# Attention's first norm, fronts, rotations and maxima placed in the first feed-forward's last two batches, and no filling periods

## The reference

```python
x = x + 0.5 * ffn(layernorm(x), ...)     # 2 shared and 8 routed experts, top 2 of 8, capacity 1280
x = x + attn(layernorm(x), ...)          # 16 heads of 64, rotary + Fourier terms, softmax
x = x + 0.5 * ffn(layernorm(x), ...)     # same weights as the first

# in attn, with scale = 64 ** -0.5:
q = q * cos + rotate_half(q) * sin + fenc
k = k * cos + rotate_half(k) * sin + fenc
out = softmax(q @ k.T * scale) @ v        # per head
return out_of_all_heads @ w_out.T + b_out

# in ffn, for every expert:
h = silu(x @ gate.T) * (x @ up.T)         # times the token's share for a routed expert
y += h @ down.T
```

## Time and profile before

| | |
|---|---|
| median of 3 runs | 1315.5 us (1313.26 to 1315.73) |
| the profiled execution | 1315.65 us, its span 1313.9 us |
| busy share | PE 97%, DVE 64%, ACT 47%, POOL 67% |
| granted TensorE clock, mean | 0.987 of full |

### The profile page before, as it was taken

One profiled execution on the slowest core, in us unless ns is written; L12 is line 12 of the kernel. 1 busy time (PEld: TensorE's weight loads), 2 busy tenths in 40 slices (PEclk: granted clock), 3 DMA queues, 4 the chain that ended last, 5 costly groups with the idle time before them and its releaser, 6 DMA issues.

```text
span 1313.9 us, 21618 instructions
## 1 busy us (share of the span) xinstructions
PE 1268.6 (97%) x7858; PEld 790.6 (60%) x7858; DVE 840.1 (64%) x1352; ACT 614.2 (47%) x917; POOL 883.0 (67%) x652
## 2 busy tenths in 40 slices
PE   5999998699999999999999999999999999999998
PEld 3666665456565656666565656565565655666665
DVE  6656646876666666666666666677786664565632
ACT  3443532255545455545545554545545444443422
POOL 0443444678797888798888888788888862443343
PEclk9999999699999999999999999999999999999999
DMA  5344040223233232323232323323232321442240
GB/s 164 129 177 125 6 130 16 48 42 70 55 66 58 54 70 50 74 50 74 49 74 50 70 54 65 59 54 70 50 74 50 73 34 18 146 137 81 66 153 17
DMA packets 118681, 95.40 MB, mean 73 GB/s; under 512 B 75760, under 2 KB 85008, under 8 KB 118320
## 3 DMA queue, kind: packets, MB, share of 16 engines
q1 hardware_dynamic: 118576, 94.01, 29.8%
HBM read 57.53 MB, written 2.88 MB: 46 GB/s over the span
## 4 chain that ended last, share of the span: by engine, by line
PE 91%; DVE 5%; issue 2%; ACT 1%; DMA 1%; POOL 0%; SPq 0%; DVEq 0%; ACTq 0%
PE banks L1028 17%; PE banks L450 16%; PE banks L1011 13%; PE banks L463 10%; PE banks L1043 7%; PE banks L987 7%; PE banks L952 6%; PE banks L1016 4%; PE banks L1052 4%; PE banks L971 3%; PE banks L994 1%; DVE neg_max L1201 1%; PE banks L412 1%; PE banks L405 1%; PE banks L476 1%
## 5 line engine op out<-in xcount | busy, mean ns | idle before, releaser
L1201 DVE TENSOR_REDUCE neg_max<-banks 128x2 f32<-128x1024 f32 x256 | 313.2, 1224 | 103.1 <-PE banks L987 96.8
L1125 ACT ACTIVATE work<-banks 128x1024 f32<-128x1024 f32 x256 | 250.2, 1025 | 166.6 <-PE banks L1016 166.6
L1303 POOL TENSOR_TENSOR turn<-turn,side_turned 128x512 f32<-128x512 f32 x128 | 160.6, 1275 | 132.4 <-DMA side_turned<-side 132.3
L1028 PE MATMUL banks<-work 128*64 128x512 f32 x1024 | 233.9, 599 | 0.0
L1297 POOL TENSOR_TENSOR turn<-turn,fenc 128x512 f32<-128x512 f32 x128 | 161.9, 1287 | 14.9 <-DVE side L1194 10.9
L1308 POOL TENSOR_TENSOR qk_l<-turn,qk_h 128x512 fp32r<-128x512 f32 x128 | 162.0, 1287 | 0.9 <-ACT qk_h L1130 0.9
L1313 POOL TENSOR_TENSOR work<-work 128x1024 f32<-128x1024 f32 x64 | 152.8, 2387 | 11.2 <-PE banks L1028 11.2
L1028 PEld LDWEIGHTS banks<-work 128*64 128x64 f32 x1024 | 67.8, 136 | 132.9 <-issue 110.1
L987 PE MATMUL banks<-qk_h 64*128 64x512 f32 x512 | 118.0, 455 | 13.2 <-DVE neg_max L1201 10.2
L796 POOL TENSOR_TENSOR turn<-turn,work 128x512 f32<-128x512 f32 x56 | 72.2, 1294 | 87.1 <-DVE turn L717 87.1
L796 POOL TENSOR_TENSOR o_raw<-o_raw,work 128x512 f32<-128x512 f32 x52 | 66.8, 1288 | 89.2 <-DVE o_raw L717 89.2
(11 more groups left out here) (169 smaller groups left out, 2364.6 us busy)
## 6 DMA issues: line engine op xcount, KB each, us to landing
work<-share SPq DMA_DIRECT2D x32, 1024.0 KB, 9.3
side_turned<-side SPq DMA_DIRECT2D x256, 128.0 KB, 3.1
rec_all<-rec_d SPq DMA_DIRECT2D x128, 128.0 KB, 3.3
x_tok<-in_x SPq DMA_DIRECT2D x8, 256.0 KB, 6.1
out<-x_tok SPq DMA_DIRECT2D x8, 256.0 KB, 9.2
work<-in_w_gate_up SPq DMA_DIRECT2D x1, 1280.0 KB, 7.8
work<-in_w_qk SPq DMA_DIRECT2D x1, 1024.0 KB, 9.5
den_d<-den_rows SPq DMA_DIRECT2D x64, 4.0 KB
```

Source lines behind the costliest of these rows:

```text
L1028: ins = nc.tensor.matmul(O[OWN[h], :], v_all[:, kt, n * DH:(n + 1) * DH], pt[:, g % 2, kt, h * T:(h + 1) * T], start=(kt == 0), stop=(kt = ...
L1125: nc.scalar.activation(pt[:, g % 2, kt, :], S[kt].rearrange("p h q -> p (h q)"), ACT.Exp, scale=QSCALE).then_inc(s["probs"], 1)
L1201: nc.vector.tensor_reduce(neg_max[:, g % 2, qt::DH], M2, AX.X, ALU.max, negate=True).then_inc(s["maxes"], 1)
L1303: nc.gpsimd.tensor_tensor(turn[:, g % 2, part], turn[:, g % 2, part], side_turned[:, part], ALU.add).then_inc(done, 1)
```

## The change

The tables move the early work, new ones are added, the three filling periods leave `PERIODS`, and GpSimd gets a hook as well. The set of `qk_h`/`qk_l` that a head pair uses is moved by one (`sets`), and the first feed-forward keeps its fronts the other way round, so that its last chunk leaves `x2_hi` and `x2_lo` to attention; `hid` buffers move from `turn[:, 1]` to `work`. The norm of batches 1 to 5 (20 tiles) is made in the hooks, that of batches 6 and 7 (8 tiles) in periods 4 to 12 (`END_AT`).

```diff
-JOIN_NORM_AT = {46: (0,), 47: (1, 2), 48: (3, 4, 5), 49: (6, 7), 50: (8, 9), 51: (10, 11), 53: (12, 13), 54: (14, 15)}
+JOIN_NORM_AT = {53: (0,), 54: (1, 2), 55: (3, 4, 5), 56: (6, 7), 57: (8, 9), 58: (10, 11), 59: (12, 13), 60: (14, 15)}
...
-        LATER = (B - 1) * TT
+        LATER = 5 * TT
...
-            FILL_FROM = -2 * PAIRS
-            EARLY_NORM_AT = {0: range(0, 4), 1: range(4, 7), 2: range(7, 10), 3: range(10, 13), 4: range(13, 16)}
-            EARLY_FRONT, EARLY_K, EARLY_Q = 5, 7, 8
-            PERIODS = range(-3, N)
-            STATS_AT, SMALL_AT = (-2, -1), (0, 1, 2, 3)
+            PERIODS = range(0, N)
+            QK_FROM, V_FROM = -48, -14
+            EARLY_NORM_AT = {-14: range(0, 4), -13: range(4, 7), -12: range(7, 10), -11: range(10, 13), -10: range(13, 16)}
+            EARLY_FRONT_AT = -9
+            EARLY_PART_AT = {-8: (0, K), -7: (0, Q), -5: (1, K), -4: (1, Q), 9: (2, K), 10: (2, Q)}
+            EARLY_MAXIMA_AT, EARLY_TURN_AT, EARLY_VALUES_AT = (4, 5, 6, 7), 8, (11, 12, 13)
+            EARLY_HIGH_AT = {-1: (0, K), 1: (0, Q), 9: (1, K), 10: (1, Q)}
+            STATS_AT = {-6: range(0, 5), -3: range(5, 10), -2: range(10, 15), -1: range(15, 20)}
+            SMALL_AT = {0: (1, 2), 1: (3, 4), 2: (5, 6), 11: range(7, 11), 12: range(11, LN_STAGES)}
+            END_AT = {4: (0,), 5: (1, 2), 6: (3, 4), 7: (5, 6), 8: (7, 8), 9: (9, 10), 10: (11, 12), 12: (13, 14, 15)}
...
             def early_act(act, k):
-                if FILL_FROM <= k < FILL_FROM + 2 * PAIRS and k % 2 == 0:
-                    qk_high(act, (k - FILL_FROM) // 2)
+                if k >= QK_FROM and (k - QK_FROM) % 4 == 0 and (k - QK_FROM) // 4 < PAIRS:
+                    qk_high(act, (k - QK_FROM) // 4)
...
             def early_dve(dve, k):
+                if k >= QK_FROM and (k - QK_FROM) % 4 == 0 and (k - QK_FROM) // 4 < PAIRS:
+                    qk_low(dve, (k - QK_FROM) // 4)
...
                 if tail is None:
                     pe.wait_ge(ffn1["x_done"], B)
+                    maxima(1, 0)
+                    maxima(1, 1)
                     for p in PERIODS:
                         period(p)
...
+                if early is not None:
+                    if early == -6:
+                        pool.wait_ge(fenc_ready, 1)
+                        fourier_part(0, K, s["early_roped"], 1)
...
+                    elif early == 8:
+                        turned_part(1, K, s["k_sum"], 1)
+                    elif early == 9:
+                        turned_part(1, Q, s["q_sum"], 2)
+                    return
+                low(1, K, s["k_high"])
+                low(1, Q, s["q_high"]).then_inc(s["low"], 1)
+                fourier_part(2, K, s["early_roped"], 1)
+                fourier_part(2, Q, s["roped"], 2)
                 for p in PERIODS:
                     period(p)
```

More of the change, by code:

```diff
@@ L379, in in_sets @@
             def in_sets(b):
[L380 removed]
+                return b // CB % 2 == 1
             def xh(b):
@@ new lines, in early_act, with high, copy_values @@
+                if k in EARLY_VALUES_AT:
+                    copy_values(act, EARLY_VALUES_AT.index(k) - len(EARLY_VALUES_AT))
+            def high(act, g, part):
+                act.wait_ge(s["k_sum" if part == K else "q_sum"], g + 1)
+                nc.scalar.activation(qk_h[:, sets(g), part], turn[:, g % 2, part], ACT.Copy)\
+                  .then_inc(s["k_high" if part == K else "q_high"], 1)
+            def copy_values(act, p):
+                b, half, t = value_tile(p)
+                act.wait_ge(s["v_ps"], p + 4)
+                at_least(act, s["o_ps"], (b - 1) * PAIRS + (half + 1) * TT)
+                nc.scalar.activation(v_all[:, t, half * T:(half + 1) * T], W, ACT.Copy).then_inc(s["v_ready"], 1)
@@ new lines, in statistics, with small_step @@
+            def statistics(dve, n, stats_of, first):
+                steps.mark(nc.vector.bn_stats(stats_of[:, n, :], x_tok[:, first + n // TT, n % TT, :]))
+            def small_step(n, size, mean_of, rs_of, shift_of):
+                if n < LN_STAGES - 1:
+                    norm_small(steps, n, size)
+                else:
+                    steps.wait()
+                    nc.vector.scalar_tensor_tensor(shift_of[:], mean_of[:], -1.0, rs_of[:], ALU.mult,
+                                                   ALU.mult).then_inc(s["norms"], 1)
@@ new lines, in early_dve @@
+                if k in EARLY_MAXIMA_AT:
+                    qt = EARLY_MAXIMA_AT.index(k)
+                    dve.wait_ge(s["max_ps"], qt + 1)
+                    maxima_of(0, qt, banks[:, 6:8, :]).then_inc(s["maxes"], 1)
+                if k == EARLY_TURN_AT:
+                    dve.wait_ge(s["shift_ps"], 1)
+                    spread(0, W[:, 0:P]).then_inc(s["shift_ready"], 1)
+                for n in STATS_AT.get(k, ()):
+                    if n % TT == 0:
+                        dve.wait_ge(ffn1["x_done"], 2 + n // TT)
+                    statistics(dve, n, stats_all, 1)
@@ L1222, in residual, with end_norm @@
                     dve.wait_ge(s["y_done"], g + 1)
[L1224 to L1243 removed]
+                def end_norm(p):
+                    for n in END_AT.get(p, ()):
+                        if n == 0:
+                            for t in range(CT):
+                                statistics(dve, t, stats_c, B - CB)
+                        else:
+                            small_step(n, CT, mean_c, rs_c, shift_end)
                 def period(p):
@@ L1390, in sync @@
                     return
+                for g in range(3):
+                    turn_partitions(g)
                 for p in PERIODS:
```

209 lines of the change are left out of this document (119 added, 90 removed).

## The result

The changed kernel takes 1319.22 us (median of 18 runs, 1315.15 to 1322.29), the kernel before 1315.18 (18 runs on the same chip, 1312.61 to 1317.4). The ratio is 1.0029, 95% interval 1.0018 to 1.0039: slower, 4.0 us. The profiled execution has a span of 1318.2 us against 1313.9, 4.3 more, so its trace can stand for the medians. The forecast was 1316.4, no change within 0.2%. The time is 2.8 us above it: inside the wide range of 1310.5 to 1322, outside the forecast's own 1314 to 1318.1, and on the side, slower than 1318.1, that had been given 0.34. Two executions in all, one of qk_later (2521 us, the traced one, its matmuls at half rate) and one of before_join53 (4396 us), are left out of every median and ratio.

The account below looks back on a forecast made before the run. The prediction took TensorE, with 91% of the chain of waits, as the bound. Its terms, -20.1 + 2.9 + 10.4 + 4.9 + 1.2 + 1.6 = +0.9 us, gave 1316.4 us, range 1310.5 to 1322.

Parts of the forecast that it names:

- Part 3: Feed-forward, period 22: the first qk_high waits for the load of w_v and delays the stream, +10.4 us.
- Rival (a): The load of w_v is there or its wait is hidden, so the wait costs 0: 1306.0 us, chance 0.05.
- rival (d): TensorE's restart behind the load wait costs in full, 12.5 us: 1318.5 us, chance 0.10.
- Parts 2 and 5: Feed-forward: work moved onto TensorE, +2.9 us, and small losses such as copies, rotation and a late gated, +1.2 us.
- rival (c): VectorE becomes the bound in batches 6 and 7, gated slips by over two units: 1320.8 us, chance 0.23.
- Part 4: End of the feed-forward: projections, rotations and blocked small steps delay batch 7's residual relative to silu(79), +4.9 us.
- X: Mark: the end of batch 7's residual; 224.05 us before the change, forecast at 243.5.
- Part 1: From X to T: skipped filling periods save 20.1 us, leaving a distance of 23.2 us.
- T: Mark: the moment pair 2's maxima are turned; 267.28 us before the change, forecast about 23 us behind X.
- rival (b): The clock comes back to 2.4 GHz between X and T, with a faster restart: 1312.5 us, chance 0.17.
- the prediction's three signs of being wrong: ScalarE's wait under 8 us; TensorE idle times over 3 us between units 60 and 79; X to T outside 20 to 26.
- Part 6: Attention: six small steps of the 8-tile norm in period 5 cost +1.48, JOIN_NORM_AT keeps its cost; +1.6 us in all.

Follow-up runs that it names:

- qk_later: The changed kernel with the copies of w_qk (qk_high, qk_low) begun in period 28 instead of 22: 1307.05 us, ratio 0.9939; measured again 1311.24 us, ratio 0.9952.
- before_join53: The kernel before with only the second feed-forward's norm steps (JOIN_NORM_AT) moved from periods 46 to 54 to periods 53 to 60: 1317.88 us, ratio 1.0012.
- before_qk22: The kernel before with only the copies of the query and key weights moved to periods 22 to 50 from 54 to 68: 1325.56 us, ratio 1.0076.
- tail_steps_earlier: The changed kernel with stages 7 to 15 of the 20-tile norm issued at k = 3 to 8 instead of 11 and 12: 1315.91 us, ratio 1.0012.
- spread_steps: The changed kernel with the eight-tile norm at most one stage a period and the joining norm's first periods thinned out: 1316.05 us, ratio 1.0001.
- no_end_norm: The changed kernel without the eight-tile norm of batches 6 and 7, so its result is wrong: 1316.39 us, ratio 1.0001.
- own_wait_for_v: The changed kernel with the load of w_v on its own semaphore, so the first qk_high waits for w_qk alone: 1317.36 us, ratio 1.0022.
- best1: The changed kernel with QK_FROM -42 and both norms one stage a period, in periods 4 to 21 and 23 to 40: 1305.29 us, ratio 0.9917.
- best2: best1 with the 20-tile norm's stages placed as in tail_steps_earlier: 1303.63 us, ratio 0.9906.

## Why the prediction was right or wrong

**Part 3, the wait**, was right in mechanism and place: ScalarE's 10.90 us, the landing of `w_v`, half clock behind it. The delay is 9.19 us instead of 10.4; 0.85 of the difference is the load, which landed at 90.35 instead of 91.2. The last link of the working was wrong. It had TensorE restart with time to spare and then wait for `gated(24)`; the windows from the restart to the transposes behind `gate_up(26)` (window, length, TensorE's busy time (x count), granted clock, DMA share, GB/s), in the changed kernel and then in before_qk22, have no idle time at all:

```profile
91.40:96.44 5.04, 5.04 (x14) 0.72 0.00 0
```

```profile
91.59:97.92 6.33, 6.33 (x14) 0.56 0.00 0
```

Before, this stretch takes 87.25 - 83.23 = 4.02 us. So the 9.19 are 8.17 of a later start and 1.02 of slow matmuls, and in before_qk22 the same step costs 10.67 at this place, 8.36 and 2.31: what the 1.2 GHz behind the wait costs differs by 1.3 us from kernel to kernel. That 10.4 lies between the two is in part luck. before_qk22 and, by its times, qk_later_again show that the delay reaches the end. Rival (a) is out; rival (d), a restart that costs in full (12.5 us), was met by neither kernel.

**Parts 2 and 5, the longer feed-forward**, were too small: 4.1 us forecast. From the transposes behind `gate_up(26)` to `silu(79)` the windows have (window, length, TensorE's busy time (x count), granted clock, DMA share, GB/s), for the changed kernel and then for the kernel before:

```profile
96.44:233.04 136.60, 133.10 (x520) 1.00 0.24 70
```

```profile
87.25:217.89 130.64, 128.99 (x505) 1.00 0.24 70
```

That is +5.96: 4.11 of busy TensorE in place of 2.9, and 1.85 more of idle time in place of 1.2 (3.50 us in four pieces, the largest 1.72 in front of a front's transposes, where it was 0.94 before). The 15 new matmuls are those that the forecast counted; the maxima cost more than it took for them. `down` at the end of three periods, the first without a pair of maxima behind it, the second with one:

```profile
217.41 1.02 PE L464 MATMUL banks<-o_raw,down_w 128*128 128x512 f32 x2
219.66 1.02 PE L464 MATMUL banks<-o_raw,down_w 128*128 128x512 f32 x2
222.53 1.02 PE L464 MATMUL banks<-work,down_w 128*128 128x512 f32 x2
```

A period of 2.25 us becomes one of 2.87, so a pair between `down` and `gate_up` costs 0.62 us, not the 0.34 of the earlier trace rows, where it stands between other maxima and scores. Four pairs make 1.1 of the 1.2 us missed. No `gated` was late enough to stop TensorE for longer, so rival (c), VectorE as the bound in batches 6 and 7, did not occur, though the time came out near its 1320.8.

**Part 4, the tail**, was right: X is 11.19 us behind `silu(79)`, against 6.16 before, +5.03 where 4.9 was forecast. VectorE was held in three steps, not four or five, and tail_steps_earlier shows what that queue cost, 1.2 us, where the forecast had 1.9 of its 4.9 for it; the chain of projections and rotations was longer by as much. The Trainium skill, in "SBUF — State Buffer", section "SBUF: two separate sides", has the shared port pair held for the whole instruction by whoever is first. The traces agree, and more widely than I used it: in period 5 it is a 2.4 us instruction that holds a step of 8 elements.

**Part 1, the periods skipped**, was right: X to T is 22.42 us (23.2 forecast), 20.81 less than before. The window from X to T in the changed kernel, with the same columns:

```profile
244.23:266.65 22.42, 16.60 (x90) 0.92 0.11 23
```

The granted clock is 0.92 in the mean, so rival (b), a clock that comes back, is partly true in this execution, for under a microsecond; spread_steps and no_end_norm have the same. In others it is not: X to T is 24.3 us at 0.79 in own_wait_for_v and qk_later_again.

The parts ahead of T were forecast to sum to -0.7 and came to -0.63, by errors that cancel: -1.2 at the wait, +1.9 in the feed-forward, +0.1 at the tail, -0.7 between X and T. That this sum is right is luck in its size. None of the prediction's three signs of being wrong came (ScalarE's wait is 10.90 us, TensorE's idle time from 182 us to `silu(79)` 1.95, X to T 22.42): all three look at what stands ahead of T, and the part that failed stands behind it.

**Part 6, attention, is the step that failed.** "+1.6 us" was +5.5 between T and the last turn. Two readings in it were wrong. I priced six small steps between two pieces of VectorE's chain at +1.48, by the earlier trace rows, as if that were a property of the steps. It is one of the ways in which they can fall: in the earlier trace rows no step met the 1024 wide sum, in the changed kernel one did, and the interval is 3.1 us too long instead of 1.5. The four traces with this norm as the change has it (changed, tail_steps_earlier, own_wait_for_v, qk_later_again) have 16.41, 17.75, 14.05 and 14.04 us there, and 161.93 to 166.75 from pair 2 to 14, so its price is anything from 1.7 to 6.5 us over no_end_norm; the forecast's row, with 14.77, happens to be one of the cheaper cases. And "`JOIN_NORM_AT` only moves, its cost stays" took the price as independent of the place; pairs 46 to 62 take 213.1 us where this norm has been moved out of them (best1, best2), 214.5 to 220.4 with it inside, in kernels that differ there in nothing or in the place of a few steps. Its price, the clock's part in it included, is anything from 1.4 to 7.3 us. Of the +5.5, 4.70 are the eight-tile norm, which no_end_norm takes away and spread_steps all but 0.6 of it, 2.51 the joining norm, and -1.85 the last pair, which is a matter of the clock and not of the change: among kernels that are alike there, changed or not, it is 13.8 to 14.2 or 15.7 to 16.0. The upper bound of part 6, 3.5 us, was worked out from the same row and was too low for the same reason.

What stays open: how much of the last 1 to 2 us of each median is the mean of such meetings. Traces of one execution each differ in them more than the medians do, and I have one trace per kernel.

## What to carry to other kernels

Price a small VectorE operation by what GpSimd is doing at that moment, not by its size or by another place in the trace. The same steps took 0.12 to 0.20 us here between GpSimd's operations, 1.2 to 1.3 beside one of 512 numbers a partition and up to 2.4 beside one of 1024: a chain of dependent small steps advanced by one, sometimes two, per GpSimd instruction. Where such steps stand ahead of something that TensorE waits for, spread them one to a period; this took back four fifths of what leaving them out did. And when a copy of weights is moved earlier, look at when the last load on its semaphore lands: at period 22 the first copy cost 10 us, at period 28 nothing to be seen.

## What the runs showed of the hardware that I had not expected

TensorE's granted clock has two levels, 2.4 GHz (1.00 in the rows) and 1.2 GHz (0.50); a figure between them is the mean of a stretch that has both. It falls at idle times that are short, and not each time. In before_join53 the 1.55 and 1.02 us above are followed by three windows at 0.72, 0.50 and 0.64 of the full clock (columns: window, length, busy time (x count) of TensorE, its weight loads, VectorE, ScalarE and GpSimd, the granted clock, DMA share, GB/s):

```profile
981.00:984.00 3.00, 1.98 (x14) 1.34 (x12) 2.96 (x3) 1.02 (x1) 1.09 (x1) 0.72 0.01 2
984.00:987.00 3.00, 3.00 (x24) 1.36 (x24) 1.57 (x2) 1.02 (x1) 1.42 (x2) 0.50 0.84 173
987.00:990.00 3.00, 3.00 (x24) 1.83 (x18) 1.31 (x2) 0.38 (x1) 1.35 (x2) 0.64 0.03 7
```

From 984 to 990 us the mean is 0.57, so by estimate 2.6 us are lost; the interval is 19.28 us, 2.4 more than the 16.86 of the changed kernel for the same meeting. There the clock stays full behind idle times of 1.81 and 1.02 us, and so it does in period 5 behind 1.35 and 1.03 us:

```profile
323.00:326.00 3.00, 1.65 (x13) 1.22 (x14) 3.00 (x4) 0.28 (x1) 1.51 (x1) 1.00 0.44 87
326.00:329.00 3.00, 1.97 (x16) 0.93 (x12) 2.60 (x3) 1.26 (x2) 1.45 (x2) 1.00 0.17 38
```

The last pair is like the first of these. TensorE before the change, with two windows of it:

```profile
1076.03 0.69 PE L987 MATMUL banks<-qk_h 64*128 64x512 f32 x2 [1.91 <-DVE neg_max L1201]
```

```profile
1075.00:1078.00 3.00, 1.97 (x18) 0.84 (x22) 2.21 (x3) 0.19 (x1) 1.27 (x1) 0.70 0.00 0
1078.00:1081.00 3.00, 3.00 (x30) 1.71 (x24) 1.51 (x2) 0.45 (x2) 0.00 (x0) 0.74 0.00 0
```

It takes 15.66 us; in the changed kernel the same stretch is at full clock and takes 13.81. Between X and T, too, it decides who keeps a gain. In own_wait_for_v the two windows from 250 to 254 us are at half clock,

```profile
250.00:252.00 2.00, 0.71 (x4) 0.00 (x0) 1.23 (x1) 1.67 (x3) 0.05 (x1) 0.50 0.00 0
252.00:254.00 2.00, 1.97 (x5) 1.60 (x6) 0.69 (x1) 0.39 (x1) 2.00 (x2) 0.50 0.00 0
```

where the changed kernel has

```profile
250.00:252.00 2.00, 2.00 (x14) 1.30 (x10) 0.07 (x1) 1.14 (x2) 0.00 (x0) 0.68 0.00 0
252.00:254.00 2.00, 0.67 (x5) 0.55 (x4) 1.46 (x2) 1.95 (x3) 0.49 (x1) 1.00 0.00 0
```

and so 1.9 us gained at the load were lost again before T: for the same 90 matmuls from X to T TensorE is busy 18.55 us instead of 16.60.
